# Routing stage of a metaformer kernel: tokens transposed in place during the top-eight search, probabilities four blocks per PSUM bank, activation tables loaded at other places

## What is computed

```python
def _L0_ffn_ref(x, gate_w, gate_b, weight1, weight2):      # x: 16 x 3600 x 64
    logits = jnp.einsum('bsd,ed->bse', x, gate_w) + gate_b
    probs = jax.nn.softmax(logits, axis=1)                 # over the tokens
    vals, idx = jax.lax.top_k(probs.transpose(0, 2, 1), K) # K = 8
    ...
    gathered = jnp.take_along_axis(x, flat_idx[:, :, None], axis=1)
    gathered = gathered.reshape(Bn, K, E, Dn)
    pooled = jnp.einsum('bked,bke->bed', gathered, topv)
    h = jnp.concatenate([pooled.transpose(1, 0, 2), ones], axis=-1)
    h = jax.nn.gelu(jnp.einsum('ebd,edh->ebh', h, weight1), approximate=False)
    ...
```

## Time and profile before

| | us |
|---|---|
| median of 3 runs (lowest, highest) | 4550.24 (4546.56, 4555.64) |
| profiled execution, its own time | 4550.77 |
| its span, first to last instruction | 4549.0 |
| busy: PE / PEld / DVE / ACT / POOL | 4387.5 / 2754.4 / 1351.7 / 1460.7 / 101.2 |
| mean granted PE clock | 0.969 |

### The profile page before, as it was taken

One profiled execution on the slowest core, in us unless ns is written; L12 is line 12 of the kernel. 1 busy time (PEld: TensorE's weight loads), 2 busy tenths in 40 slices (PEclk: granted clock), 3 DMA queues, 4 the chain that ended last, 5 costly groups with the idle time before them and its releaser, 6 DMA issues.

```text
span 4549.0 us, 106098 instructions
## 1 busy us (share of the span) xinstructions
PE 4387.5 (96%) x42695; PEld 2754.4 (61%) x42695; DVE 1351.7 (30%) x2531; ACT 1460.7 (32%) x5350; POOL 101.2 (2%) x163
## 2 busy tenths in 40 slices
PE   7999999998789999999999989999999999999999
PEld 2899999983335399999995333333333333333333
DVE  3555533335542655543334520000000000000000
ACT  5002344443332301234444223333333333333333
POOL 1000000000000000000000000000000000000000
PEclk8999999999886899999999999999999999999999
DMA  5000000022234500000004400000000000000000
GB/s 133 15 0 0 0 0 0 0 60 71 66 92 117 160 0 0 0 0 0 0 0 137 112 14 9 17 17 17 17 9 17 17 17 17 10 16 17 17 17 13
DMA packets 146728, 139.18 MB, mean 31 GB/s; under 512 B 79550, under 2 KB 146142, under 8 KB 146654
## 3 DMA queue, kind: packets, MB, share of 16 engines
q1 hardware_dynamic: 146654, 138.21, 11.9%
HBM read 79.18 MB, written 58.98 MB: 30 GB/s over the span
## 4 chain that ended last, share of the span: by engine, by line
PE 94%; DVE 3%; ACT 1%; issue 1%; DMA 0%; POOL 0%; SPq 0%; DVEq 0%; ACTq 0%; POOLq 0%; PEldq 0%
PE ps L755 22%; PE ps L707 20%; PE ps L685 17%; PE ps L836 16%; PE ps L750 3%; PE ps L513 3%; PE ps L534 2%; PE ps L524 1%; PE ps L573 1%; PE ps L658 1%; PE ps L737 1%; PE ps L505 1%; DVE rstd L1063 1%; PE ps L727 1%; PE ps L729 1%
## 5 line engine op out<-in xcount | busy, mean ns | idle before, releaser
L755 PE MATMUL ps<-idle 128*32 128x512 bf16 (+1 forms) x5894 | 1638.5, 340 | 0.8 <-DVE xl L1042 0.8
L836 PEld LDWEIGHTS ps<-xl,vt 65*32 65x32 f32 x14400 | 520.9, 108 | 1163.7 <-ACT xl L1035 1111.5
L1035 ACT ACTIVATE xl<-ps 64x16 f32<-64x16 f32 x3600 | 637.2, 177 | 1251.8 <-PE ps L836 1251.8
L707 PE MATMUL ps<-xl,taps 128*128 128x128 f32 (+2 forms) x7880 | 914.1, 279 | 4.7 <-DVE xl L1232 4.7
L707 PEld LDWEIGHTS ps<-xl,taps 128*128 128x128 f32 x7880 | 913.6, 191 | 5.4 <-issue 5.3
L836 PE MATMUL ps<-xl,vt 65*32 65x16 f32 x14400 | 871.2, 193 | 7.9
L685 PE MATMUL ps<-split 128*128 128x400 f32 x4140 | 781.2, 352 | 12.8 <-DVE split L1227 12.8
L685 PEld LDWEIGHTS ps<-split 128*128 128x128 f32 x4140 | 779.2, 190 | 16.6 <-issue 15.2
L1300 DVE TENSOR_TENSOR xl<-xl 64x480 f32<-64x480 f32 x120 | 116.4, 970 | 1774.0 <-PEq L833 887.7
L906 ACT ACTIVATE img<-xl 128x144 f32 x788 | 365.8, 464 | 549.2 <-DVE xl L1209 549.2
L1209 DVE SCALAR_TENSOR_TENSOR xl<-ps,img 128x144 f32<-128x144 f32 x788 | 323.3, 410 | 589.8 <-PE ps L707 589.8
(11 more groups left out here) (139 smaller groups left out, 1828.4 us busy)
## 6 DMA issues: line engine op xcount, KB each, us to landing
ring<-in_x_dram SPq DMA_DIRECT2D x144, 200.0 KB, 3.7
x_dram<-sums SPq DMA_DIRECT2D x144, 200.0 KB, 3.2
t_dram<-sums SPq DMA_DIRECT2D x72, 200.0 KB, 3.6
ring<-t_dram SPq DMA_DIRECT2D x72, 200.0 KB, 3.8
ring<-x_dram SPq DMA_DIRECT2D x72, 200.0 KB, 3.7
xl<-x_dram SPq DMA_DIRECT2D x30, 480.0 KB, 6.3
out_dram<-xl SPq DMA_DIRECT2D x30, 480.0 KB, 4.7
img<-in_L_ffn_weight_dram SPq DMA_DIRECT2D x4, 512.0 KB
```

What stands on the lines that cost most here:

```text
L707: last = pe.matmul(acc[:, :, lo:hi], taps[:, (k * NO + d + 2) * 128:(k * NO + d + 3) * 128], column[h][:, :, lo + d:hi + d], start=(n == 0 ...
L755: pe.matmul(PS[bank][0:32, 0:n], idle[:, 0:32], idle[:, 0:n], start=True, stop=True)
L836: last = pe.matmul(PS[s][c * 32:(c + 1) * 32, t * B:(t + 1) * B], vt[:, c * 32:(c + 1) * 32], prev, start=False, stop=True, skip_group_che ...
L1035: act.activation(yb[0:64, s % 2, :, t], PS[s % 2][0:64, t * B:(t + 1) * B], ACT.Sigmoid).then_inc(step_y, 1)
```

## The change

Four things, all in layer 0's routing; the rest of the kernel is untouched, though line numbers shift.

- **Tokens.** The 60 blocks of 120 tokens (2 x 30) are transposed on their own in 15 batches of four blocks, one bank each (ps2, ps3, ps6, ps7 in turn), right after the logits. ACT copies a batch (120 x 512) back into `xl`, where block `b` of the result takes columns `128 b` to `128 b + 127`. The batches go from the last block down, so that the result, which is wider, never covers a block not yet read; `xl` grows by 480 columns. ACT does batches 0 to 4 ahead of Exp (`BEFORE_EXP = 5`) and 5 to 14 after it.
- **Probabilities.** The 30 blocks are transposed in eight parts of four or three, one bank each (ps4, ps5), again from the last down, and copied in one piece; then a part's matmuls follow in a row. So the second half of `spare` is kept and scaled first.
- **Tables.** Exp is asked for right after `take_std`, and Sqrt (in group 3: Gelu) after ACT's last copy of probabilities, before it waits for the pooled sums.
- **Order on PE.** In a group: all batches of tokens, then parts 0 and 1 of probabilities, then matmuls of part 0, transposes of part 2, matmuls of part 1, and so on.

```diff
+        def first_block(m):
+            return 2 * NTC - XT_BLOCKS * (m + 1)
+        def by_token(v, c):
+            return xl[0:TC, (v * NTC + c) * 128:(v * NTC + c + 1) * 128]
...
         def pooling(pe, g):
-            for c in range(NTC + 2):
-                if c in (0, NTC // 2):
-                    pe.wait_ge(prob_ready, g * 2 + (c // (NTC // 2) + 1))
...
-                    pe.transpose(bank[0:TC, 0:128], slots[:, c // (NTC // 2), HB, (c % (NTC // 2)) * TC:(c % (NTC // 2) + 1) * TC], ident[:, :])
-                    for v in range(2):
-                        last = pe.transpose(bank[0:TC, 128 + v * 128:256 + v * 128],
-                                            xl[:, v * S + c * TC:v * S + (c + 1) * TC], ident[:, :])
...
+            pe.wait_ge(ln[1].std, g + 1)
+            for m in range(XT_BATCHES):
+                bank = PS[XT_BANKS[m % len(XT_BANKS)]]
+                if m >= len(XT_BANKS):
+                    pe.wait_ge(xt_kept, g * XT_BATCHES + m - len(XT_BANKS) + 1)
+                for q in range(XT_BLOCKS - 1, -1, -1):
+                    b = first_block(m) + q
+                    last = pe.transpose(bank[0:TC, q * 128:(q + 1) * 128], xl[:, b * TC:(b + 1) * TC], ident[:, :])
+                last.then_inc(xt_tr, 1)
+            def turn(i):
+                z = 1 - i // HALF_PARTS
+                if i % HALF_PARTS == 0:
+                    pe.wait_ge(prob_ready, g * 2 + i // HALF_PARTS + 1)
...
+                if i >= 2:
+                    pe.wait_ge(tt_ready[i % 2], g * (len(PARTS) // 2) + (i - 2) // 2 + 1)
+                for q, c in enumerate(PARTS[i]):
...
+            def gather(i):
+                pe.wait_ge(tt_ready[i % 2], g * (len(PARTS) // 2) + i // 2 + 1)
+                pe.wait_ge(xt_kept, g * XT_BATCHES + batch_of(PARTS[i][0]) + 1)
...
+            turn(0)
+            for i in range(len(PARTS)):
+                if i + 1 < len(PARTS):
+                    turn(i + 1)
+                gather(i)
...
                     take_std(act, i, g)
+                    act.activation(warm[:, :], ones[0:1, 0:1], ACT.Exp)
                     route(act, g)
...
-            act.activation(warm[:, :], ones[0:1, 0:1], ACT.Exp)
+            for m in range(BEFORE_EXP):
+                keep_by_token(act, g, m)
             act.wait_ge(top_found, g + 1)
...
-            for c in range(1, NTC, 2):
-                take_transposed(act, g, c, lambda o, a: act.activation(o, a, ACT.Copy))
-            act.wait_ge(pool_mm, g * NTC + NTC)
+            for m in range(BEFORE_EXP, XT_BATCHES):
+                keep_by_token(act, g, m)
+            for i in range(1, len(PARTS), 2):
+                take_transposed(act, g, i, lambda o, a: act.activation(o, a, ACT.Copy))
+            act.activation(warm[:, :], ones[0:1, 0:1], ACT.Sqrt if g + 1 < NG else ACT.Gelu)
+            act.wait_ge(pool_mm, (g + 1) * len(PARTS))
...
+            keep_top(1)
+            scale(1)
+            take(0)
             keep_top(0)
+            take(2)
             scale(0)
-            for c in range(0, NTC, 2):
-                take_transposed(dve, g, c, lambda o, a: dve.tensor_copy(o, a))
...
+            for i in range(4, len(PARTS), 2):
+                take(i)
```

More of the change, by code:

```diff
@@ L286, in metaformer, with batch_of @@
         KEPT = NCH + 4
+        XT_BANKS = (2, 3, 6, 7)
+        PT_BANKS = (4, 5)
+        PARTS = [range(26, 30), range(22, 26), range(18, 22), range(15, 18), range(11, 15), range(7, 11), range(3, 7), range(0, 3)]
+        HALF_PARTS = len(PARTS) // 2
+        assert sorted(c for part in PARTS for c in part) == list(range(NTC))
+        def first_block(m):
+            return 2 * NTC - XT_BLOCKS * (m + 1)
+        def by_token(v, c):
+            return xl[0:TC, (v * NTC + c) * 128:(v * NTC + c + 1) * 128]
+        def batch_of(c):
+            return (2 * NTC - 1 - c) // XT_BLOCKS
         def token_spread_bank(i, n, v):
@@ new lines, in turn @@
+            def turn(i):
+                z = 1 - i // HALF_PARTS
+                if i % HALF_PARTS == 0:
+                    pe.wait_ge(prob_ready, g * 2 + i // HALF_PARTS + 1)
+                if i == 0:
+                    pe.wait_ge(ln[1].taken, (g + 1) * NCH)
+                if i >= 2:
+                    pe.wait_ge(tt_ready[i % 2], g * (len(PARTS) // 2) + (i - 2) // 2 + 1)
+                for q, c in enumerate(PARTS[i]):
+                    a = c * TC - z * SLOT
+                    last = pe.transpose(PS[PT_BANKS[i % 2]][0:TC, q * 128:(q + 1) * 128], slots[:, z, HB, a:a + TC], ident[:, :])
+                last.then_inc(transposed, 1)
@@ new lines, in gather @@
+            def gather(i):
+                pe.wait_ge(tt_ready[i % 2], g * (len(PARTS) // 2) + i // 2 + 1)
+                pe.wait_ge(xt_kept, g * XT_BATCHES + batch_of(PARTS[i][0]) + 1)
+                for q, c in enumerate(PARTS[i]):
+                    o = (i % 2 * XT_BLOCKS + q) * 128
+                    for v in range(2):
+                        last = pe.matmul(PS[0][v * 64:(v + 1) * 64, 0:128], tt[:, o + v * 64:o + (v + 1) * 64], by_token(v, c),
+                                         start=(i == 0 and q == 0), stop=(c == PARTS[-1][-1]))
+                last.then_inc(pool_mm, 1)
@@ L998, in route, with keep_by_token, take_transposed @@
             own(act)
-        def take_transposed(eng, g, c, move):
-            eng.wait_ge(transposed, g * NTC + (c + 1))
-            if c >= RING:
-                eng.wait_ge(pool_mm, g * NTC + (c - RING + 1))
-            move(tt[:, (c % RING) * 384:(c % RING + 1) * 384], PS[5 + c % RING][0:TC, 0:384]).then_inc(tt_ready[c % 2], 1)
+        BEFORE_EXP = 5
+        def keep_by_token(act, g, m):
+            b = first_block(m)
+            act.wait_ge(xt_tr, g * XT_BATCHES + m + 1)
+            act.activation(xl[0:TC, b * 128:(b + XT_BLOCKS) * 128], PS[XT_BANKS[m % len(XT_BANKS)]][0:TC, 0:XT_BLOCKS * 128], ACT.Copy
+                           ).then_inc(xt_kept, 1)
+        def take_transposed(eng, g, i, move):
+            n, o = len(PARTS[i]) * 128, i % 2 * XT_BLOCKS * 128
+            eng.wait_ge(transposed, g * len(PARTS) + i + 1)
+            if i >= 2:
+                eng.wait_ge(pool_mm, g * len(PARTS) + i - 1)
+            move(tt[:, o:o + n], PS[PT_BANKS[i % 2]][0:TC, 0:n]).then_inc(tt_ready[i % 2], 1)
         @block.scalar
```

30 lines of the change are left out of this document (9 added, 21 removed).

## The result

The changed kernel takes 4467.5 us (median of 4 runs, 4466.3 to 4471.6) against 4548.4 us (4 runs, 4545.9 to 4555.6) in the same comparison. The ratio is 0.9827, with a 95% interval from 0.9813 to 0.9841: a gain of 80.9 us in the medians. The forecast was 4479, with 4467 to 4505 as the range, so the direction is right and the time lies just inside the range's lower end. The profiled run took 4466.3 us, its span is 4464.5 us, 84.5 less than before.

A forecast was written before the change was run, and what follows sets the result against it. TensorE (PE) was taken to bound the kernel, on the last-ending chain for 94% of the span. Poolings' 69.3 us plus tables' 2.2 made 71.5 off 4550.24, forecast 4479 us; range 4467 to 4505.

The forecast's parts named there:

- The poolings: Layer 0's routing, first probability transpose through pooled copy: four groups fall from 125.1 to 55.8 us, a gain of 69.3.
- T: Moment in each group when VectorE's search has given the first half of the probabilities; 1146.94 us in group 1 before.
- The tightest point: In the pooling, the probabilities' second half is ready at about T + 5.3 us; PE asks for it at T + 5.6.
- The price of a change: In the pooling, each PE change between transposes and matmuls costs 0.155 us at the full clock, 0.19 at the low.
- The start after T: Token batches left after Exp end before T at the full clock; at the low one pooling starts up to 1.8 us late.
- The clock: In the search PE's clock still falls, at 1140 to 1143.5 us, and returns between T - 1 and T + 2.
- the clock is half the story: Old poolings: the same 210 instructions take 26.6 us at a mean clock of 0.93 and 40.5 us at 0.55.
- The direct term: Activation tables: no load ahead of Sqrt saves 2.2 us in three groups; a load before the pooled copy costs 1.4.
- One: Poolings: transposes don't bring the clock back; 4522 us with all groups low, 4490 with one; chance 0.25.
- Two: Search: the clock never falls, as the new gap is 5.3 us and not 12.4; 4474 us; chance 0.05.
- Three: Early token transposes aren't hidden because PE and ACT take turns; 24 us a group, 4525 us; chance 0.03.
- Four: The low clock reaches the next group's norm and logits; two such groups cost 91 us, giving 4570; chance 0.02.

The follow-up runs named there:

- the single blocks: Changed kernel with the probabilities in 30 parts of one block instead of eight of three or four: one run, 4505.1 us.
- the second profile: The changed kernel, with no further edit, profiled again and timed: 4470.3 us, ratio to the kernel before 0.9833.
- the run with the tokens late: Changed kernel with all token batches behind the wait for the first half of the probabilities, no copies ahead of Exp: one run, 4507.7 us.
- the version with added matmuls: Changed kernel with eight copies ahead of Exp, Sqrt or Gelu requested after pooled values are written, and matmuls on zeros in PE's gaps: 4467.6 us, ratio 0.9825.

## Why the prediction was right, point by point

**The poolings.** The sum was 125.1 to 55.8 us, the copy of the pooled sums included, a gain of 69.3; measured is 72.2 less from T to the end, and 0.9 lost on the copies. Step by step: 12.4 us at the full clock became 12.34 with a stall of 0.35 for the first copy, against 0.4. The tightest point held too: the second half of the probabilities was ready at 1130.36, and PE began on it at 1130.94. The sum of the prices held, though not each term: the terms add up to 12.2 where 12.4 was taken, and they count 15 changes where PE's row has 13. The price of a change was tested by the single blocks: 44 more of them cost 7.65 us a group, 0.74 of it in longer waits for copies, which leaves 0.157 us each against 0.155.

**The start after T.** I had the last batches end by T at the full clock, and up to T + 1.8 at the low one. Both profiles fit that. In group 1 PE resumed at 1121.28, T - 3.4 as forecast, and ran its 24 transposes without a gap. In the first profile 13 to 22 of the 24 ran at the low clock, which put the start at T + 0.7 to T + 1.6; in the second all did, and it came at T + 1.8. ACT's copies did not hold PE there: the eleventh, for which the last batch waits, ended at 1123.87, and that batch began at 1124.99. The T + 13.6 for the end was a choice within the bounds; measured are 13.3 and 14.4 in the mean.

**The clock.** Forecast: it falls at 1140 to 1143.5 on the old time axis (T - 6.9 to T - 3.4) and returns between T - 1 and T + 2. In group 1 it fell at T - 3.7 and returned at T - 0.3, in the second profile it fell at T - 4.6 and returned at T + 2.2. The returns of the first profile lie inside the bounds in all groups (T - 0.5 to T + 1.3), those of the second at the edge or just past it (T + 2.0 to T + 2.7). But "the clock is half the story" was too much: the run with 50 added matmuls puts the clock's share at 22 of the pooling's 125 us, or of the 72 gained.

**Tables.** The direct term was 2.2 us forward, 1.4 back; measured 2.16 and 0.88. The 1.4 rests on a slip: 0.85 + 0.64 and two changes of 0.155 are 1.80 and not 1.75, so about 0.3 a group was due, and 0.27 came, of which 0.05 was there before. As a whole the term was mis-sized. Taking the early Sqrt out of the changed kernel costs 12 to 14 us, with 24 us at the low clock in group 2 that both profiles without it show and none with it does. The sum had no term for this. That the wait of 0.72 us is what brings it is argued and not shown: the same wait does nothing in the other groups.

**The rest.** 72.3 us in the routing against the sum's 71.5 is closer than the working deserves: the terms for poolings and tables came to 73.5, and 1.2 us were lost elsewhere; the clock, for one, was low for 3.4 us at the start of the first norm. The second profile has 75.2, of which 68.1 lie from T to the end and about 6 in the norms. The time moved by 80.9, and the 9 us between them are the code outside, where these runs show nothing beyond chance. It had 5 us in the bounds; two profiles of the same kernel lie 7 us apart there. The range's lower end (4467) was half a microsecond from being passed, so that the time fell inside it is luck too. The range should have allowed some 10 us for this, on both sides.

**Rivals.** One (transposes don't bring the clock back) fell: in group 1 the clock returned after 3.0 us of transposes and nothing else, and in the run with the tokens late 2.9 to 6.0 us into a row of 60. The rule of the Trainium skill (TensorE: Matmul & The Clock Gate, Part 4: PE-mode transpose), that the full clock doesn't engage for transposes, does not hold for these 120x128 fp32 ones; the measurement decides. What kept the 18 transposes at the start at 0.226 us each stays open: the profile lists no low clock there. Two (the clock never falls) fell, but for the version with added matmuls, where the three undisturbed groups end at T + 12.45. Three (no overlap) fell: the last copy comes at T + 1.7. (Its time should have read 4520 and not 4525: 24 us a group are 96 in all.) Four, the low clock in the next norm and logits, came in the changed kernel only as the short stretches of 3.4 to 6.8 us that were there before. As a mechanism it is real: the version without early Sqrt has 23.9 us of it and pays some 11 us in that group's period, against the 45 a group that the rival had. I had put its cause at the wrong place, behind the pooling, where this stretch begins in the spreads, ahead of the logits.

## What to carry to other kernels

Work that needs only what is there already belongs ahead of the wait for what isn't. Here that was worth 31 us. Part of this is the tokens' own time (25.7 us at the full clock, an estimate from 240 transposes of 0.107 us), and part is that PE's clock is back, or nearly so, when the result is ready. Keep kinds of PE instructions together when a change between them costs as much as one of them (0.155 us here; 176 more changes, with the stalls that small copies brought, cost 31 us). Ask for an activation table where ACT idles and nobody is next in line: a request ahead of a short copy cost 0.9 us in each of four groups of the old pooling, more than it gained. And when the clock's low stretches move a run by 10 us, take a gain of a few us from a profile of the stage, not from the time.

## What was not expected of the hardware

- PE's clock stayed at the lower level for 23.9 us in which PE was busy throughout (spreads of 32x400 and logits of 64x400 tiles), in two profiles at the same place, while in the other groups the same steps ran at the full clock.
- With 24 transposes behind the search the low stretch lasted 3.4 or 6.8 us. With 12, and a wait behind them, it lasted 10.2 us in three of four groups.
- In untouched code two profiles of one kernel differed by 10 us over 990, as the clock was low for 34 us in one and 55 in the other.
- ACT's copies of 120x512 in a row follow each other at 0.52 us although each is listed with 0.60.
